# Expert steps: the pair's update and outputs move ahead of the expert's gate and up products in slots two, four and six

## What is computed

```python
xn = _layernorm(x)
# attention branch: gated linear attention, 8 heads, key width 128, value width 64
state = a_t * state + k_t v_t^T          # a_t = sigmoid((xn @ Wg + bg) / 16), one per head and token
out_t = q_t @ state
attn = (out * sigmoid(xn @ Wog)) @ Wo
# expert branch: 64 experts, top 8 of 4 groups per token, at most 256 tokens per expert
g = einsum("ech,ehi->eci", buf, w_gate)  # buf: the expert's tokens, 256 x 256
u = einsum("ech,ehi->eci", buf, w_up)
y = einsum("eci,eih->ech", silu(g) * u, w_down)
out = x + attn + scatter_add(y * weight)
```

## Time and profile before

| what | value |
|---|---|
| time, median of 3 runs | 1263.7 us (1263.62 to 1264.16) |
| the profiled execution, its own time | 1266.82 us, its span 1265.1 us |
| granted TensorE clock in it | 1.00 |
| TensorE matmul / weight load busy | 98% / 86% of the span |
| VectorE / ScalarE / GpSimd busy | 77% / 49% / 39% |
| the eight expert steps | from about 530 to about 1205 us |

### The profile page before, as it was taken

One profiled execution on the slowest core, in us unless ns is written; L12 is line 12 of the kernel. 1 busy time (PEld: TensorE's weight loads), 2 busy tenths in 40 slices (PEclk: granted clock), 3 DMA queues, 4 the chain that ended last, 5 costly groups with the idle time before them and its releaser, 6 DMA issues.

```text
span 1265.1 us, 28662 instructions
## 1 busy us (share of the span) xinstructions
PE 1237.9 (98%) x9910; PEld 1092.2 (86%) x9910; DVE 976.6 (77%) x2343; ACT 624.3 (49%) x1319; POOL 487.4 (39%) x377
## 2 busy tenths in 40 slices
PE   7899999999999999999999999999999999999999
PEld 6788888887888888799899998989989999889987
DVE  6997878889797659878688687786885877868844
ACT  6675756666574544344444444444444444434432
POOL 2110111011001027237467385474574754845620
PEclk9999999999999999999999999999999999999999
DMA  6576534354352322357486575674774765748665
GB/s 241 170 250 200 188 110 156 122 190 158 121 171 60 111 75 84 95 145 186 105 198 165 130 178 136 150 181 106 188 171 121 172 155 137 193 104 191 162 194 183
DMA packets 124920, 194.68 MB, mean 154 GB/s; under 512 B 12016, under 2 KB 98608, under 8 KB 124592
## 3 DMA queue, kind: packets, MB, share of 16 engines
q1 hardware_dynamic: 94384, 147.99, 36.1%
q0 software_dynamic: 30464, 45.83, 19.7%
HBM read 148.62 MB, written 57.74 MB: 163 GB/s over the span
## 4 chain that ended last, share of the span: by engine, by line
PE 76%; DVE 16%; issue 5%; ACT 2%; another core or an unknown queue 0%; DVEq 0%; DMA 0%; ACTq 0%
PE bank L793 21%; PE bank L808 7%; PE bank L905 7%; PE bank L937 7%; PE bank L845 6%; PE bank L825 5%; PE bank L877 3%; PE bank L863 3%; PE bank L866 3%; PE bank L948 3%; PE bank L836 3%; DVE Dt L1506 3%; PE bank L889 2%; PE bank L927 2%; DVE At L1527 2%
## 5 line engine op out<-in xcount | busy, mean ns | idle before, releaser
L635 POOL DMA_INDIRECT acc<-arena,idx_all x128 | 224.3, 1752 | 149.4 <-DMA acc<-res 54.1
L627 POOL DMA_INDIRECT arena<-table,idx_all x132 | 163.6, 1240 | 153.8 <-ACT share L1160 96.5
L793 PE MATMUL bank<-xp,wq 128*128 128x512 f32 x768 | 208.4, 406 | 0.0
L793 PE MATMUL bank<-xp,wk 128*128 128x512 f32 x768 | 202.2, 398 | 0.0
L793 PEld LDWEIGHTS bank<-xp,wk 128*128 128x128 f32 x768 | 138.5, 188 | 29.3 <-DVE wk L1416 0.4
L793 PEld LDWEIGHTS bank<-xp,wq 128*128 128x128 f32 x768 | 136.6, 189 | 25.4 <-issue 0.8
L1506 DVE TENSOR_TENSOR_SCAN Dt<-decay,eye_b 128x512 f32<-128x512 f32 x128 | 157.7, 1233 | 0.0
L845 PE MATMUL bank<-qT,kT 128*128 128x128 f32 x1024 | 136.2, 275 | 1.8 <-DVE At L1527 1.4
L1136 ACT ACTIVATE kT<-bank 128x512 f32<-128x512 f32 x128 | 76.7, 599 | 118.0 <-PE bank L793 102.2
L845 PEld LDWEIGHTS bank<-qT,kT 128*128 128x128 f32 x1024 | 125.2, 192 | 3.3 <-DVE At L1527 1.6
L1136 ACT ACTIVATE qT<-bank 128x512 f32<-128x512 f32 x128 | 76.9, 601 | 85.4 <-PE bank L793 64.7
(11 more groups left out here) (174 smaller groups left out, 2317.1 us busy)
## 6 DMA issues: line engine op xcount, KB each, us to landing
decay<-decay_dram SPq DMA_DIRECT2D x64, 512.0 KB
carry<-decay_dram SPq DMA_DIRECT2D x60, 512.0 KB
arena<-in_L_attn_x_dram SPq DMA_DIRECT2D x16, 512.0 KB, 4.5
table<-arena SPq DMA_DIRECT2D x16, 512.0 KB, 3.2
xT_dram<-arena SPq DMA_DIRECT2D x16, 512.0 KB, 3.0
arena<-in_L_ffn_w_gate_dram SPq DMA_DIRECT2D x64, 128.0 KB
arena<-in_L_ffn_w_up_dram SPq DMA_DIRECT2D x64, 128.0 KB
arena<-in_L_ffn_w_down_dram SPq DMA_DIRECT2D x64, 128.0 KB
```

The source lines that it names most:

```text
L627: pool.indirect_dma_start(out=xg[:, e % 2, j, :], out_offset=None, in_=table[:, :], in_offset=bass.IndirectOffsetOnAxis(ap=idx_all[:, e, j ...
L635: pool.indirect_dma_start(out=acc[:, :], out_offset=bass.IndirectOffsetOnAxis(ap=idx_all[:, e, j:j + 1], axis=0), in_=yb[:, e % 2, j, :], ...
L793: last = mm(to[:, :], w[:, part, k, h * DK:(h + 1) * DK], xp[:, other, k, :], start=(k + i == 0), stop=(k == KD - 1 and i == 2))
```

## The change

In slots 2, 4 and 6 of the expert steps, `update` and `outputs` are issued ahead of `expert_hidden` on TensorE, and `update_back` behind it. That is the order that slot 8 has already. On ScalarE `update_copy` moves ahead of `expert_gate`. On VectorE `pair_gated` and `pair_state` move ahead of `expert_hidden`, `weights_low_e`, `hidden_low` and `down_low`; `outs_low` stays last. No instruction is added or removed. Odd slots and slot 8 keep their order.

```diff
@@ TensorE, beside
-                if kind == "experts" and s > 0 and place == (2 if s < H else 4):
+                if kind == "experts" and s > 0 and place == (2 if s % 2 else 4):
                     expert_hidden(c, s - 1)
@@ ScalarE, beside
                 if kind == "experts" and s > 0 and place == 2:
-                    if s == H:
+                    if s % 2 == 0:
                         update_copy(c, s // 2 - 1)
                     expert_gate(c, s - 1)
@@ ScalarE, step
                     beside(c, kind, s, 2)
-                    if s % 2 == 0 and s < H and kind == "experts":
-                        update_copy(c, s // 2 - 1)
                     beside(c, kind, s, 3)
@@ VectorE, beside
-                    if place == 2 and s < H:
+                    if place == (2 if s % 2 else 4) and s < H:
                         expert_hidden(c, s - 1)
                         weights_low_e(c, s)
                         if s < H - 1:
```

## The result

The changed kernel takes 1271.94 us (median of 6 runs, 1269.11 to 1273.85) beside 1263.66 us for the kernel before (6 runs, 1262.19 to 1265.87): the medians lie 8.3 us apart. The ratio, taken from all runs, is 1.0061, 95% interval 1.0047 to 1.0074, which makes 7.7 us (5.9 to 9.4). The forecast was 7.4 us. The profiled execution took 1272.2 us, its span is 1270.6 us.

What follows compares the result with a forecast made beforehand. The prediction took TensorE to set the pace, with VectorE at 79% near enough for its queue order to matter. Seams of 1.2 us plus waits of 6.2 made 7.4, from 1263.7 to 1271.1 us, range 1264.6 to 1275.2.

Steps and rivals of the forecast that it cites:

- TensorE's seams: TensorE in slots 2, 4 and 6: the new neighbours cost 0.05 us in each of 24 slots, 1.2 us, bounds 0 to 2.4.
- The chain in slot 7: VectorE's late queue makes TensorE's gate and up in slot 7 start at 5.77 instead of 5.27, 0.58 us with restart.
- L1566's wait for L889: Sign in the profile after: VectorE's state sum waits about 0.7 us for the turned-back sum in slots 2, 4 and 6.
- What holds the expert's instructions: VectorE: the expert's five instructions stand behind L1566, which waits for the turned-back sum, so they start in the next slot.
- The step sum: Waits of 0.58 us in slot 7 and 0.20 in slot 8: 0.78 us per step, 6.2 us in 8 steps.
- Only slot 7: Slots 3 and 5 show no wait: the output gate's product, worth 1.40 us, covers VectorE's lateness with 0.9 us lead.
- A wait at slot 7's down product: TensorE in slot 7: the down product may wait up to 0.1 us for L1609, inside the wait behind it, not added.
- Edits at no price: ScalarE's earlier copy, earlier update and outputs, and SyncE's loads some 2.5 us later cost nothing; failed cover: up to 2.5 us per slot.
- Rival 1: VectorE's queue has unseen slack, no wait appears on TensorE, seams alone are paid: 1264.9 us; chance 0.15.
- Rival 2: Faster: the gap ahead of VectorE's L1549 swallows late events, saving 4 us of TensorE's waits: 1260.9 us; chance 0.08.
- Rival 3: Slower still: late events reach TensorE in full where no lead is left, 4 x 1 us more: 1275.1 us; chance 0.15.

Runs made afterwards that it cites:

- VectorE's old order: TensorE and ScalarE in the changed kernel's order, VectorE's queue left in the kernel before's order: 1289.77 us, ratio 1.0230, +29.3 us.
- the low outputs early: Changed kernel with ScalarE's copy of the gated outputs ahead of the sigmoid and VectorE's low outputs ahead of the state sum: 1263.22 us, ratio 1.0022.
- the kernel after again: The changed kernel itself, unaltered, timed again in the second group beside the kernel before: 1270.51 us, ratio 1.0058, +8.1 us.
- the third group: Runs on one chip: changed kernel with the turned-back sum behind the outputs, 1264.78 us; kernel before with VectorE ahead, 1260.62; kernel before, median 1260.52 (17 runs).
- the kernel before with VectorE ahead: Kernel before with ScalarE's weights' copy (L1167) ahead of `update_copy` in slots 2, 4 and 6: 1261.57 us, ratio 0.9994; in the third group 1260.62, 0.9999.

## Why the prediction was right, point by point

- **TensorE's seams.** Forecast 0.05 us in each of 24 slots, measured 0.06. Keys' product into the update 1.49, as forecast; gate and up behind the outputs 1.54 for 1.52. The runs of slots 2 and 4 alone agree, +1.2 us, with an interval of 0.1 to 2.5. The rule of the Trainium skill ("TensorE: Matmul & The Clock Gate", "Back-to-back issue gap"), by which the order would cost nothing, did not hold by this much.
- **The chain in slot 7.** Forecast and measured starts, in us from slot 7's L836: state sum 0.27 and 0.28, first expert instruction 0.87 and 0.88, L1568 3.07 and 3.07, L1612 4.94 and 4.95, L937 5.77 and 5.77, L1519 9.98 and 9.97, L877 10.72 and 10.71. It worked because each distance was taken start to start from a row in which the same instruction followed the same one. One sign was off in size: L1566's wait for L889 shows as 0.42 us of idle time, not about 0.7; the 0.7 was the distance from L889's start.
- **What holds the expert's instructions.** The prediction puts them into the next slot because they stand behind L1566. That is the wait that ends last, but by little: with L889 ahead of gate and up they still start 0.62 into the next slot, since the sigmoid isn't out before, and 0.51 of the 0.76 us of waits remain. The prediction mentions the sigmoid only to say that it is out by then; it is, by a quarter of a microsecond.
- **The step sum.** 0.78 us forecast for slots 7 and 8, measured 0.76 (0.58 + 0.18).
- **Only slot 7.** Right in the profile of after (slots 3 and 5 take 0.01 us more) and shown by taking the cover away. For slot 3 that is clean; slot 5 has more in it. That the lateness is over behind a covered slot holds at this size; with more of it it is false, as VectorE's old order showed in slots 4 and 6.
- **A wait at slot 7's down product.** Forecast up to 0.1, inside the one behind it. L948 starts 3.18 into the slot instead of 3.16, at 0.94 us long instead of 0.88. It is inside.
- **Edits at no price.** ScalarE's move was not run alone; in the profile of after its copy ends 3.1 us before the sigmoid starts. L1167 waits for weights once, 0.6 us, in the profile of after, and once, 1.2 us, in that of before. SyncE's later loads cost nothing that shows: they start as late in the run with the low outputs early, which loses 2.8 us.
- **Rival 1, no wait appears:** fell. The kernel with the low outputs early (+2.8) comes near it; the change doesn't.
- **Rival 2, faster:** half its mechanism is there, L1547 has its gap of 2.2 us, and in that profile none of the late events shows at it. But they then show at L1564, and nothing is won.
- **Rival 3, slower still:** its term was an extra 1 us for each late event. Measured, an event ahead of slot 7 costs 1.4 us in either order, so the extra is near nothing.
- **Where the rest is.** Eight steps explain 7.7 us of the 8.3 and 8.1 measured, intervals of 6 to 9.4 and 5 to 9.6. The remainder is inside them and I don't assign it. The number of late events, which differs from run to run, is one part of the scatter. Another is TensorE's clock, in the step that builds the lists. Two stretches from the trace of the turned-back sum right behind the outputs, then the same two from that of the kernel before, profiled again (columns as in the earlier trace rows; the clock is the third number from the end):

```profile
520.00:522.00 2.00, 0.21 (x4) 0.17 (x4) 2.00 (x4) 0.60 (x1) 0.00 (x0) 0.99 0.00 0
522.00:524.00 2.00, 2.00 (x22) 2.00 (x22) 2.00 (x4) 0.00 (x0) 0.00 (x0) 0.50 0.00 0
```

```profile
520.00:522.00 2.00, 0.32 (x6) 0.32 (x8) 2.00 (x3) 0.55 (x1) 0.00 (x0) 1.00 0.00 0
522.00:524.00 2.00, 2.00 (x37) 1.83 (x31) 2.00 (x5) 0.00 (x0) 0.00 (x0) 1.00 0.00 0
```

TensorE waits 1.8 us for VectorE in both of these executions. In the first the granted clock then falls to 0.50, which is 1.2 of 2.4 GHz, and the part of the step around it takes 18.6 us instead of 17.2; the profile of the kernel after again has the same fall. It is outside the expert steps and can strike any of these kernels. Of the 17 runs of before in the third group 11 lie at 1260.3 to 1260.7 and 6 at 1261.5 to 1261.8, with none between; three of the six have a mean clock of 0.994, and none of the eleven is below 0.996. That the second level is this fall of the clock is likely and not shown. What sends the late events is open; no run here isolated it.

No kernel of this study beat the kernel before; the nearest changed order (slots 2 and 4 alone) is 1.2 us behind, and the kernel before with VectorE ahead equals it.

## What to carry to other kernels

Before moving a product ahead of another one on the bound engine, ask which instruction of the neighbour's in-order queue waits for what now comes last, and list all that stands behind it: here the wait for the turned sum, and behind it the later gate and up products themselves, put five instructions of an expert into the next slot. Then compare, slot by slot, the lead that each consumer has: a slot with one more product for the bound engine hid what the next one paid in full. A control without the change is needed when such a product is moved: here the move cost 4.7 us by itself. If the wait can't be removed, work that doesn't depend on it goes ahead of it (+2.8 us remained here instead of +8.1).

## What was not expected of the hardware

- A group of matmuls costs by its neighbours as well: the keys' product takes 1.40 or 1.49 us, gate and up 1.42 in slot 7, and 1.51, 1.52 or 1.54 with the half-width matmuls of the update or the outputs beside them. One order of the same groups is 0.06 us dearer than the other in 6.2, the same in every step of the traces; in the times of the runs 16 such slots make +1.2 us, just clear of nothing (0.1 to 2.5).
- After a wait for a semaphore, TensorE's group takes 1.66 us instead of 1.58 (L937) and 0.94 instead of 0.88 (L948), in the kernels of this study that wait there; L948 does so even where its wait is too short to be listed. In these kernels a wait costs its length and about 0.08.
- VectorE can start an instruction that needs TensorE's result some 1.1 to 2.1 us later than it does in the other steps, in some executions only: at L1549 before, at L1564 after. A trace doesn't say whether the signal or the start is late.
